# A second half's z that is copied out as it is and taken through silu one chunk later, on the scalar engine of a Mamba and mixture-of-experts kernel

## The reference

```python
xz = hidden_states @ in_proj_w.T            # 128 -> 2 x 256
x, z = jnp.split(xz, 2, axis=-1)
...                                         # causal convolution of x, 4 taps, + conv_b
x = jax.nn.silu(xc)
...                                         # B, C, delta = softplus(...) from x
s = s * dA + (d_t * u_t)[..., None] * B_t[:, :, None, :]   # dA = exp(d_t * A), 16 states
y_t = jnp.einsum('bhdn,bhn->bhd', s, C_t)
...
y = y + x * Dskip
y = y * jax.nn.silu(z)                      # the gate: the only reader of z
out = y @ out_proj_w.T
```

## Time and profile before

| | |
|---|---|
| median of 3 runs | 1044.19 us |
| lowest and highest | 1042.48 and 1044.27 us |
| the profiled execution's own time | 1043.7 us |
| its span, first to last instruction | 1041.9 us |
| busy: DVE, PE, POOL, ACT | 94%, 90%, 85%, 72% |
| mean granted TensorE clock | 0.971 of full speed |

### The profile page before, as it was taken

How to read it: one execution, slowest core, us unless ns; L and a number is a source line. 1 busy time by engine, 2 the same in 40 slices (tenths; PEclk the granted TensorE clock), 3 DMA queues, 4 the chain that set the end, 5 groups by cost and what they waited for, 6 DMA issues and landing times.

```text
span 1041.9 us, 12066 instructions
## 1 busy us (share of the span) xinstructions
PE 939.1 (90%) x3541; PEld 430.9 (41%) x3541; DVE 980.4 (94%) x1339; ACT 749.7 (72%) x1199; POOL 889.4 (85%) x820
## 2 busy tenths in 40 slices
PE   6888687789999999999998999999999999999777
PEld 3433233234444444444444444444444444444233
DVE  7789988899999999999999999999999999999998
ACT  5667556478787888788777878877787978778532
POOL 5548888888889898988989979897998989898997
PEclk9989798799999999999999999999999999999988
DMA  9775453356534634655364355545445355544795
GB/s 265 206 197 130 109 121 74 90 147 146 110 64 98 135 80 100 144 112 102 76 138 92 80 134 109 102 100 118 102 90 133 86 104 109 101 90 94 130 225 111
DMA packets 76061, 123.78 MB, mean 119 GB/s; under 512 B 9390, under 2 KB 39004, under 8 KB 75996
## 3 DMA queue, kind: packets, MB, share of 16 engines
q1 hardware_dynamic: 64640, 93.55, 40.8%
q0 software_dynamic: 11008, 29.44, 13.4%
q10 hardware_dynamic: 348, 0.03, 0.0%
HBM read 17.99 MB, written 21.10 MB: 38 GB/s over the span
## 4 chain that ended last, share of the span: by engine, by line
PE 27%; ACT 13%; POOL 9%; issue 8%; DVE 7%; DMA 3%; SPq 0%; POOLq 0%; DVEq 0%; ACTq 0%
POOL s_sb L672 6%; DVE u_sb L1053 4%; PE bank L1305 4%; PE bank L1212 4%; PE bank L1312 4%; PE bank L1275 3%; PE bank L1324 3%; ACT bank L888 3%; PE bank L1232 3%; PE bank L1272 3%; DVE s_sb L1122 2%; PE bank L1223 2%; DMA dd<-neg_hi 1%; DMA dsp<-dd 1%; ACT xn L826 1%
## 5 line engine op out<-in xcount | busy, mean ns | idle before, releaser
L672 POOL TENSOR_TENSOR s_sb<-s_sb,c_of 128x512 f32<-128x512 f32 x491 | 653.5, 1458 | 76.7 <-DVE s_sb L1122 71.7
L1122 DVE TENSOR_TENSOR_SCAN s_sb<-bank,u_sb 128x512 f32<-128x512 f32 x511 | 619.1, 1211 | 26.9 <-ACT bank L888 19.6
L888 ACT ACTIVATE bank<-bank,a_neg 128x510 f32<-128x510 f32 x512 | 331.0, 662 | 156.8 <-PE bank L1312 154.7
L1053 DVE TENSOR_TENSOR u_sb<-bank,b_of 128x512 f32<-128x512 f32 x512 | 341.1, 666 | 6.0 <-PE bank L1305 5.8
L1312 PE MATMUL bank<-dsp,sel_d 128*128 128x512 f32 x512 | 315.6, 616 | 22.8 <-DVE s_sb L1122 22.6
L1305 PE MATMUL bank<-dsp,sel_d 128*128 128x512 f32 x512 | 219.0, 428 | 31.3 <-DVE u_sb L1053 21.2
L1312 PEld LDWEIGHTS bank<-dsp,sel_d 128*128 128x128 f32 x512 | 98.4, 192 | 194.1 <-DVE s_sb L1122 111.8
L1305 PEld LDWEIGHTS bank<-dsp,sel_d 128*128 128x128 f32 x512 | 99.1, 194 | 125.2 <-DVE u_sb L1053 69.3
L1324 PE MATMUL bank<-s_sb,con 128*32 128x512 f32 x992 | 138.3, 630 | 2.7 <-POOL s_sb L672 2.7
L1212 PE MATMUL bank<-xnT,wx 128*128 128x512 f32 x256 | 131.6, 616 | 0.0
L641 POOL DMA_INDIRECT moe<-xn x64 | 64.9, 1014 | 15.2 <-issue 9.4
(11 more groups left out here) (153 smaller groups left out, 1031.7 us busy)
## 6 DMA issues: line engine op xcount, KB each, us to landing
b_of<-bc SPq DMA_DIRECT2D x64, 256.0 KB, 5.4
c_of<-bc SPq DMA_DIRECT2D x64, 256.0 KB, 5.9
dd<-neg_hi POOLq DMA_DIRECT2D x32, 512.0 KB, 4.7
dsp<-neg_hi SPq DMA_DIRECT2D x64, 256.0 KB
dsp<-dd SPq DMA_DIRECT2D x64, 256.0 KB
expert_in<-fill SPq DMA_DIRECT2D x16, 260.0 KB, 5.6
xn<-expert_in SPq DMA_DIRECT2D x8, 520.0 KB, 5.2
moe<-fill SPq DMA_DIRECT2D x8, 512.0 KB, 7.0
```

The source lines that it names most:

```text
L672: pool.tensor_tensor(s_now, s_now, c_of[:, hf, hh, :], ALU.mult).then_inc(S["p_ready"], 1)
L888: act.activation(d, d, ACT.Exp, scale=a_neg[:, k:k + 1]).then_inc(S["decay_ready"], 1)
L1053: dve.tensor_tensor(u_sb[:, w % U_RING, :], du_ps[w % 2][:, :], b_of[:, hf, head_of(w), :], ALU.mult).then_inc(S["u_ready"], 1)
L1122: dve.tensor_tensor_scan(s_sb[:, w % S_RING, :], decay_of(w)[:, :], u_sb[:, w % U_RING, :], 0.0, ALU.mult, ALU.add).then_inc(S["scan_done" ...
```

## The change

ACT no longer takes silu of z1 in slot 16. For chunks 1 to 14 it copies the tile as it is into `zs` in slot 15 (`copy_z`, a `Copy` from PSUM, ahead of the load of tables), and takes `zs` through silu in place in the `silus` call for half 0 of the chunk after, behind that call's own two silus (`late_z`). The gates of half 1 wait for a new semaphore, `z_ready`. The table entries of z1 change from 15.5 to 15; for the last chunk's z1 the read stays half a slot ahead of x1's, with the silu where it was. Chunk 0 is not touched.

```diff
-    ("v0", 1, (6,), "act", 8), ("x1", 1, (11, 11, 12, 14), "act", 16), ("z1", 0, (13,), "act", 15.5),
+    ("v0", 1, (6,), "act", 8), ("x1", 1, (11, 11, 12, 14), "act", 16), ("z1", 0, (13,), "act", 15),
...
-    ("v0", 0, (8,), "act", 10), ("x1", 1, (8, 9, 10, 11), "act", 16), ("z1", 0, (12,), "act", 15.5),
+    ("v0", 0, (8,), "act", 10), ("x1", 1, (8, 9, 10, 11), "act", 16), ("z1", 0, (12,), "act", 15),
...
+            table = EARLY_A if of <= DVE_PARTS_TO else STAGE_A
+            x1_read = [read for name, _, _, _, read in table if name == "x1"][0]
+            return [Tile(name[:-1], of, int(name[-1]), 0, bank_, tuple(first + w for w in slots), by,
+                         first + (x1_read - 0.5 if (name, of) == ("z1", CHUNKS - 1) else read))
+                    for name, bank_, slots, by, read in table]
...
+        def wait_z(eng, ch, hf):
+
+            if hf == 1 and 0 < ch < CHUNKS - 1:
+                eng.wait_ge(S["z_ready"], ch)
...
                 pool.wait_ge(S["skip_added"], per_chunk(ch, 2, hf + 1))
+                wait_z(pool, ch, hf)
...
+            def late_z(ch, hf):
+
+                return hf == 1 and 0 < ch < CHUNKS - 1
+
+            def copy_z(ch):
+
+                wait(act, "g_ready", per_chunk(ch, 2, -2))
+                act.wait_ge(S["misc_pe"], tile_made("z", ch, 1, 0))
+                act.activation(zs_of(ch, 1), tile_bank("z", ch, 1, 0)[:, :], ACT.Copy).then_inc(S["misc_act"], 1)
+
             def silus(ch, hf):
 
-                wait(act, "g_ready", per_chunk(ch, 2, hf - 3))
-                act.wait_ge(S["misc_pe"], tile_made("z", ch, hf, 0))
-                act.activation(zs_of(ch, hf), tile_bank("z", ch, hf, 0)[:, :], ACT.Silu).then_inc(S["misc_act"], 1)
+                if not late_z(ch, hf):
+                    wait(act, "g_ready", per_chunk(ch, 2, hf - 3))
+                    act.wait_ge(S["misc_pe"], tile_made("z", ch, hf, 0))
+                    act.activation(zs_of(ch, hf), tile_bank("z", ch, hf, 0)[:, :], ACT.Silu).then_inc(S["misc_act"], 1)
                 act.wait_ge(S["misc_pe"], tile_made("x", ch, hf, 0))
                 act.activation(xs_of(ch, hf), tile_bank("x", ch, hf, 0)[:, :], ACT.Silu, bias=cb[:, hf:hf + 1]
                                ).then_inc(S["misc_act"], 1)
+                if hf == 0 and late_z(ch - 1, 1):
+                    act.wait_ge(*tile_read("z", ch - 1, 1, 0))
+                    act.activation(zs_of(ch - 1, 1), zs_of(ch - 1, 1), ACT.Silu).then_inc(S["z_ready"], 1)
                 act.preload_act_table_set("natural_log_exp_and_others")
...
                         if x.kind == "x":
                             silus(x.of, x.hf)
+                        elif x.kind == "z" and late_z(x.of, x.hf):
+                            copy_z(x.of)
...
                     dve.wait_ge(S["skip_added"], per_chunk(ch, 2, hf + 1))
+                    wait_z(dve, ch, hf)
```

More of the change, by code:

```diff
@@ L261, in bass_mamba_moe @@
             "moe_put3 moe_added0 moe_added1 moe_added2 moe_added3 moe_added4 moe_added5 moe_added6 moe_added7 moe_added8 "
-            "skip_ready last_scan last_p last_sum last_g last_proj last_out moe_added9 moe_added10 moe_added11 moe_added12 moe_added13 moe_added14 moe_added15 out_stored").split()}
+            "z_ready skip_ready last_scan last_p last_sum last_g last_proj last_out moe_added9 moe_added10 moe_added11 moe_added12 moe_added13 moe_added14 moe_added15 out_stored").split()}
         def stage_a_tiles(of):
             first = (of - 1) * SLOTS
-            return [Tile(name[:-1], of, int(name[-1]), 0, bank_, tuple(first + w for w in slots), by, first + read)
-                    for name, bank_, slots, by, read in (EARLY_A if of <= DVE_PARTS_TO else STAGE_A)]
+            table = EARLY_A if of <= DVE_PARTS_TO else STAGE_A
[3 more added lines that the diff above has]
+                    for name, bank_, slots, by, read in table]
         def start_tiles():
```

## The result

| | before | after |
|---|---|---|
| median | 1044.04 us (20 runs) | 1046.41 us (20 runs) |
| lowest and highest | 1041.60 and 1046.42 us | 1043.94 and 1048.95 us |
| profiled execution, its span | 1043.7, 1041.9 us | 1045.07, 1043.2 us |
| mean granted TensorE clock in it | 0.971 | 0.964 |

The ratio of after to before is 1.0024, with an interval of 1.0015 to 1.0033: the change costs 2.4 us (1.6 to 3.4). The changed kernel run again (after_again) gave 1.0018 [1.0006, 1.0029].

The account below looks back on a forecast made before the run. DVE was taken to bound the kernel, busy 980.4 of 1041.9 us, so only its idle time counted. 4.6 us lost to the late silu less 1.4 gained at slot 16 gave 3.2 slower, 1047.2 us, range 1043.2 to 1050.2.

Parts of the forecast that it names:

- The silu of z leaves slot 16: Ahead of scan 17, half 1: silu's 0.49 us out, copy in, limited by x1's readiness; 1.4 us gained in all.
- The rival of the whole place gained: Slot 16: x1 ready earlier than its record ends, 0.49 us gained in five more chunks; 1.6 us slower, 1045.3; chance 0.17.
- The bank free earlier and the extra waits: z1's bank freed earlier for PE, and added waits of POOL and DVE before gates: 0 each; the bank 3 us at most.
- The late silu's size: In the `silus` call of half 0, ahead of the exp of slot 8: 0.52 us more a call.
- Where it is soaked up: After slot 8: 0.52 us lost in chunks 3, 4, 6, 7, 9, 10, 12, 13; 0 in 2, 5, 8, 11, 14.
- Chunks 0 and 1: Chunk 0 gains the full 0.49 us at scan 17; chunk 1 loses 0.43 us to the late silu at slot 6.
- The waiting load: Half 1: first table load waits for x1, delaying silu of x 0.9 to 1.3 us; 17.5 us slower, 1061; chance 0.04.
- Soaked up everywhere: Slot 8's delay absorbed by later DVE waits for PE, loss only 0.4 us; 0.9 us faster, 1042.8; chance 0.17.
- Nothing given back: Chunks 5, 8, 11, 14 also lose 0.52 us each to the late silu; 5.3 us slower, 1049; chance 0.12.

Follow-up runs that it names:

- copy_only: Changed kernel without the late silu: copy in slot 15 kept, gates of half 1 multiply by z itself; 0.9989 of the kernel before (1042.4 us).
- late_only: Kernel before, silu of z1 still in slot 16, plus a plain copy of `zs` onto itself at the late silu's place; 1.0037 of the kernel before.
- load_waits: Changed kernel with one more, already fulfilled wait, so that the wait for x1 stands alone ahead of the table load; 1063.0 us, 1.0166 of the kernel before.
- late_5_8_11_14: Kernel before with the change only for z1 whose late silus fall in chunks 5, 8, 11 and 14; 0.9993 of the kernel before.
- late_3_6_9_12: Kernel before with the change only for z1 whose late silus fall in chunks 3, 6, 9 and 12; 1.0035 of the kernel before.
- late_twice: Changed kernel with each late silu followed by a copy of `zs` onto itself that waits for it; 1055.67 us, 1.0092 of the kernel before.

## Why the prediction was right, and where not

I forecast 1047.2 us, 3.2 slower, and measured are 1046.41 and 2.4. Step by step:

**The silu of z leaves slot 16: right.** 0.18 us were said for chunks 3, 6, 9 and 12 and 0.49 for chunk 0; the wait at scan 17 fell by 0.15 to 0.19 and by 0.39 in copy_only. In 2, 4, 7, 10 and in 5, 8, 11 nothing was gained, as said. The rival of the whole place gained would have needed 0.49 in the first group. Only chunk 13 has 0.03 for 0.17.

**The bank free earlier and the extra waits: 0, as said.** copy_only has both effects, and its chunks show no gain beyond the one above, but for 0.10 us in chunk 13, which is within what that chunk varies by.

**The late silu's size: right.** 0.52 us said, 0.52 us from silu of x to load, 0.48 to 0.53 us at the scan of slot 8 in all of the chunks 3 to 14. Its duration is 0.63 us; the Trainium skill's formula for an ACTIVATE ("ScalarE: Activation LUTs", What ACT_TABLE_LOAD costs) estimates 0.613.

**Where it is soaked up: right in nine chunks of twelve.** 5, 8, 11 and 14 lose nothing, because DVE waits for the spread of slot 12, whose wait fell from 0.70 to 0.20 us in chunk 8, 0.02 from the said 0.18. In 5, 11 and 14 it fell less, to 0.32, 0.47 and 0.26 us, though the chunks are as long as before all the same. 3, 4, 7, 9 and 10 lose all of it. This is the step that failed: "there is no slack ... everything moves with DVE" was read from chunk 6 and carried to its like, and in chunk 6 itself PE was waiting 0.50 us for POOL at slot 10, in chunk 12 1.00 us at slot 11. PE kept its place by this reserve, and DVE got the delay back later: in late_only its wait at the scan of slot 17 fell from 1.60 to 1.05 us in chunk 6, and in chunk 12 it got back 0.34 us by slot 14 and 0.16 at slot 17. Twice 0.5 us, 1.0 of the 1.1 by which the sum over chunks 2 to 14 was too high. The rest is chunk 13, where the delay is given back at scan 17 down to 0.2 us (0.51 to 0.20 in late_only), so that the copy has nothing to gain there: 0.19 instead of 0.35. There too PE had a reserve, 0.18 us of waiting for the DMA of `dsp` in slot 13 before and none in the changed kernel.

**Chunks 0 and 1: open.** I set -0.49 and +0.43. The wait at scan 17 of chunk 0 fell from 0.87 to 0.43 us in the changed kernel's first trace, but only to 0.76 in after_again, with 0.28 us of new idle at slot 16; and the two chunks together moved by +0.1 and +1.0 us in two traces of the same changed kernel, so its cost there can't be told from one profile.

**The rivals.** The waiting load didn't come, and load_waits gives its price. Soaked up everywhere is refuted by chunks 3, 4, 7, 9, 10 (+0.34 to 0.53 each), but a part of it, in 6 and 12, is true. Nothing given back is refuted by late_5_8_11_14.

**What wasn't foreseen at all** is the clock: a later exp at slot 8 lengthens PE's pause there, and the half clock that can follow costs three times the silu. In the traces of the changed kernel it didn't occur. The forecast was thus right by its mechanism, with the loss 1.1 us too high in known places.

None of the runs gives a version that beats the kernel before: the copy alone, which leaves the silu out, has 1.1 us to give, and wherever the late silu is free (that of z1 for 5, 6, 8, 11, 12, 14) the copy of the same z1, one chunk earlier, gains at most the 0.10 us of chunk 13, which isn't clear of that chunk's own variation.

## What to carry to other kernels

An operation moved from one place on a feeding engine to another is worth the difference of two waits of the bounding engine, and both must be read chunk by chunk: at the old place what will be late next (here x1, which left 0.18 of 0.49 us), at the new place whether a later wait of the bounding engine is released by something that doesn't move. Look for that reserve on every engine in between, not only on the bounding one: a wait of PE for POOL hid as much as a wait of DVE for PE. And cut the trace at a mark that recurs: most chunk lengths repeat to 0.05 us where whole runs scatter by 2. Before a single chunk's difference is put down to the change, look for the same difference in a trace in which that chunk wasn't touched: two of them, of 0.46 and 0.29 us, went with a clock that rose late and with a wait for a DMA.

## What the runs showed of the hardware

- A pause of PE of 2.23 us was followed by 3.4 us at a granted clock of 0.50 and cost about 1.5 us (chunks 3 and 9 of late_3_6_9_12), the same pause in the changed kernel by none; over all traces it was 3 of 12. With 1.3 us of needless matmuls in the pause it was 1.07 us and the clock held, in the trace and by the time (1.0035 to 0.9999).
- A load of tables runs ahead of a semaphore wait that its ACTIVATE carries, and stands behind one that is an instruction of its own: 0 against 1.35 us idle, 17 us over the kernel. Of two waits written ahead of one ACTIVATE it was the second that became the instruction of its own (L774 in load_waits, L763 at the copy in the changed kernel).
- A copy from SBUF onto itself that waits for the silu just before it starts 0.66 us after it (462.32 to 462.98 in late_twice), 0.03 us after the silu's end. The two silus ahead don't depend on each other, and the second starts 0.57 us after the first, 0.11 us before its end. So the wait for one's own predecessor on ACT cost 0.1 us here.
